# Edge layer of a four-layer graph network: the memset of an unused tile behind each of GpSimd's gathers is taken out

## The reference, cut to what matters

```python
h = maximum(layernorm(x), 0)
# _L2_gnn_ref(h, edge_index, edge_attr_64, W, b, gamma, beta):
msgs = concatenate([node_features[source], edge_features], axis=-1)   # 256 + 64 wide
msgs = silu(msgs @ W + b)
out = segment_sum(msgs, target, num_segments=n_nodes)
out = layernorm_0.001(out) * gamma + beta
x = x + out
```

## Time and profile before

| what | value |
|---|---|
| median of three runs | 7409.11 us |
| span of the profiled execution | 8931.6 us |
| span above the median | 1522.5 us |
| GpSimd busy | 5847.5 us, 65% of the span |
| TensorE matmuls busy | 5412.5 us, 61% |
| VectorE busy | 4963.7 us, 56% |
| ScalarE busy | 3871.5 us, 43% |
| granted TensorE clock, mean | 0.745 |
| DMA traffic | 894.72 MB, mean 100 GB/s |

### The profile page before, as it was taken

How to read it: one execution, slowest core, us unless ns; L and a number is a source line. 1 busy time by engine, 2 the same in 40 slices (tenths; PEclk the granted TensorE clock), 3 DMA queues, 4 the chain that set the end, 5 groups by cost and what they waited for, 6 DMA issues and landing times. The chain is left out here.

```text
span 8931.6 us, 130458 instructions
## 1 busy us (share of the span) xinstructions
PE 5412.5 (61%) x23088; PEld 4000.6 (45%) x23089; DVE 4963.7 (56%) x11653; ACT 3871.5 (43%) x9075; POOL 5847.5 (65%) x8186
## 2 busy tenths in 40 slices
PE   6442365666535656664676666658888754666665
PEld 5431244444424444443455555435555533444443
DVE  6444355555545555554677777744444445555556
ACT  2220255455424554552244444335555533454444
POOL 0555677777747777775467666657777765777774
PEclk9555677777767777776788988868888866777777
DMA  4112233333313333331466666423333323333332
GB/s 143 49 49 52 75 95 95 95 96 95 86 44 97 96 95 95 96 97 33 127 176 178 177 176 175 129 64 99 100 101 100 101 53 101 99 99 99 98 98 74
DMA packets 580940, 894.72 MB, mean 100 GB/s; under 512 B 307359, under 2 KB 357708, under 8 KB 580448
## 3 DMA queue, kind: packets, MB, share of 16 engines
q0 software_dynamic: 245984, 649.30, 26.7%
q1 hardware_dynamic: 334448, 218.84, 8.9%
q10 hardware_dynamic: 416, 25.60, 0.9%
HBM read 859.36 MB, written 59.47 MB: 103 GB/s over the span
## 5 line engine op out<-in xcount | busy, mean ns | idle before, releaser
L2002 POOL DMA_INDIRECT ad_ring<-tab_qv,ad_idx x808 | 770.7, 954 | 506.4 <-issue 217.6
L1515 POOL DMA_INDIRECT at_ring_0a<-tab_s,at_idx_0a x808 | 774.3, 958 | 430.9 <-PE at_po_0a L1680 219.2
L2396 POOL DMA_INDIRECT ae_ring<-tab_a,ae_idx x808 | 777.9, 963 | 423.0 <-PE ae_po L2553 233.7
L1515 POOL DMA_INDIRECT at_ring_0b<-tab_s,at_idx_0b x808 | 772.8, 956 | 426.7 <-PE at_po_0b L1680 213.2
L1515 POOL DMA_INDIRECT at_ring<-tab_s,at_idx x808 | 780.1, 965 | 377.6 <-PE at_po L1680 183.0
L1680 PE MATMUL at_po_0a<-at_rows_0a,at_hot_0a 128*128 128x264 f32 x1616 | 625.6, 560 | 520.8 <-ACT at_hr_0a L1780 199.8
L1680 PE MATMUL at_po_0b<-at_rows_0b,at_hot_0b 128*128 128x264 f32 x1616 | 624.3, 559 | 512.2 <-ACT at_hr_0b L1780 201.7
L1680 PE MATMUL at_po<-at_rows,at_hot 128*128 128x260 f32 x1616 | 614.5, 553 | 444.5 <-DVE acc L1566 179.0
L1680 PEld LDWEIGHTS at_po_0a<-at_rows_0a,at_hot_0a 128*128 128x128 f32 x1616 | 439.3, 282 | 670.8 <-DVE acc L1566 262.0
L1680 PEld LDWEIGHTS at_po_0b<-at_rows_0b,at_hot_0b 128*128 128x128 f32 x1616 | 438.5, 282 | 662.4 <-DVE acc L1566 264.4
L1680 PEld LDWEIGHTS at_po<-at_rows,at_hot 128*128 128x128 f32 x1616 | 435.9, 280 | 586.2 <-DVE acc L1566 225.4
(11 more groups left out here) (508 smaller groups left out, 14085.4 us busy)
## 6 DMA issues: line engine op xcount, KB each, us to landing
at_rr_0a<-relrow_d SPq DMA_DIRECT2D x102, 256.0 KB
at_rr_0b<-relrow_d SPq DMA_DIRECT2D x102, 256.0 KB
ad_rr<-relrow_d SPq DMA_DIRECT2D x102, 256.0 KB
at_rr<-relrow_s SPq DMA_DIRECT2D x102, 256.0 KB
ae_feat<-attr_pad SPq DMA_DIRECT2D x808, 32.0 KB
rnk_lrow<-lorow_f SPq DMA_DIRECT2D x98, 256.0 KB
attr_pad<-in_edge_attr_dram ACTq DMA_DIRECT2D x1, 25000.0 KB, 79.1
at_ring_0a<-tab_s,at_idx_0a POOLq DMA_INDIRECT x808
```

Source lines behind the costliest of these rows:

```text
L1515: eng.indirect_dma_start(out=ring[:, t.slot * STEP + u, :], out_offset=None, in_=table, in_offset=bass.IndirectOffsetOnAxis(ap=idx[:, t.sl ...
L2002: eng.indirect_dma_start(out=ring[:, t.slot * STEP + u, :], out_offset=None, in_=table, in_offset=bass.IndirectOffsetOnAxis(ap=idx[:, t.sl ...
L2396: eng.indirect_dma_start(out=ring[:, k, :], out_offset=None, in_=table, in_offset=bass.IndirectOffsetOnAxis(ap=idx[:, k:k + 1], axis=0))\
```

## The change

The tile `pause`, the semaphore `paused`, its wait and the 808 memsets are taken out. Nothing else is touched; gathers, their order and their other waits stay.

```diff
@@ aggregate_edges
-            pause = sb(f"ae_pause_{tag}", [P, STEP, P], F32, c)
@@
-            paused = ph.sem("ae_paused")
@@ @block.gpsimd
                     def gather(i, quads):
-                        eng.wait_ge(paused, i * STEP + STEP)
                         for q in range(quads):
                             eng.wait_ge(copied, i * (STEP // QUAD) + q + 1)
                             eng.wait_ge(summed, i * HALF + (q * 2 + 2))
@@
                                 eng.indirect_dma_start(out=ring[:, k, :], out_offset=None, in_=table,
                                                        in_offset=bass.IndirectOffsetOnAxis(ap=idx[:, k:k + 1], axis=0))\
                                     .then_inc(landed[k], 16)
-                                eng.memset(pause[:, k, :], 0.0).then_inc(paused, 1)
-
-                    eng.sem_inc(paused, STEP)
+
                     with eng.Fori(0, TURNS - 1) as i:
```

## The result

The changed kernel takes 7316.3 us (median of 4 runs, 7312.02 to 7316.78), the kernel before 7407.38 us beside it (7399.68 to 7412.71). The ratio is 0.9876, 95% interval 0.9863 to 0.9890: 91 us faster. I had forecast 7375 us, and 7335 us as the low end of the range.

What follows compares the result with a forecast made beforehand. GpSimd's gather cadence was held likelier than not to pace timed runs, though the profiled edge layer was bound by TensorE, VectorE and ScalarE. Half of 69 us, 34 us, off 7409 gave 7375 us; 8-in-10 range 7335 to 7445 us.

Steps and rivals of the forecast that it cites:

- the balance: Five edge passes: GpSimd's sequence without waits, 5767 us, nearly fills the estimated 5793 us, so GpSimd likely paces timed runs.
- "no change" rival: Edge layer: TensorE's loop paces timed runs too, GpSimd just waits 1.36 us a turn more; 7409 us, chance 0.27.
- The step: Edge layer, gather to gather on GpSimd: 1.345 to 1.26 us without the memset, 69 us over 808 gathers.
- The wait for `paused` "costs nothing": Edge layer, once a turn: it asks for memsets the same engine has done in order, so removing it gains nothing.
- Half of 69 us: Edge layer: gain between 0 and 69 us, the other engines' reserve unknown, so half was taken, 34 us.
- The 17.6 us that I had added up for TensorE: Edge layer: TensorE's four quads and sixteen transposes a turn at 2.4 GHz, without waits between engines.
- The low end: Whole kernel: 7335 us, the lower bound of the 8-in-10 range, just beyond the full gain.
- The clock rival: Seam of two edge-layer turns: longer quiet puts more of a turn at 1.2 GHz; 7435 us, slower, chance 0.23.
- a step of the clock, 56 us: Edge layer: denser TensorE raises its clock 0.81 to 0.87, 1.1 us a turn, 56 us; left out of the sum.
- Longer gathers: Edge layer: gathers without a memset between take 1.063 us, step 1.363 us, up to 7423 us; chance 0.05.
- What I said the profile would show: Edge layer: step 1.26, gap 0.30, gather 0.96 us; waits on sums about 300 us; layer within 10 us of before.
- Wrong in kind if the layer itself becomes shorter by more than 20 us: Edge layer in the profile: stated sign that the forecast is wrong in kind, a shortening of more than 20 us.

Runs made afterwards that it cites:

- second profile: The kernel before, profiled once more with no edit, after the 8931.6 us execution used for the prediction: 7396.4 us.
- all_out: Changed kernel with the memsets of the three attention passes, their tile, semaphore and waits taken out too: 7284.8 us, 0.9839.
- quad_wait: Kernel before with all memsets kept, but each quad waits for the memsets of a turn ago, not the last issued: 7361.3 us, 0.9943.
- seam_only: Changed kernel plus one memset a turn behind its last gather, and the wait for it at the next turn's start: 7341.9 us, 0.9923.
- Light_chain: Changed kernel with three of four "project" products of each edge-layer quad left out, all gathers kept: 7294.0 us, 0.9858.
- half_gathers: Changed kernel with every second gather of the edge layer left out, its rows staying zero: 7314.1 us, 0.9882.

## Why the prediction was wrong

*Who paces.* For the edge layer the balance was right. In the second profile the five passes take 5871 us from first to last gather, 104 us more than GpSimd's bare sequence of 5767 us, and in the edge layer 1126.5 us against 1087: the difference is the stall. But that GpSimd's sequence fills a pass doesn't say how near the next limit is: in the attention passes it filled them too, and the same edit bought next to nothing (all_out). The second profile has 1.5 us of waits for the sums where the first had 233.7. The "no change" rival, which rested on those waits, fell with them.

*The step.* 1.345 to 1.26 us, 69 us, was the forecast; 1.346 to 1.263 and 67 us is what came. Its parts (gap 0.16 to 0.17 behind a memset, 0.30 behind a gather) hold.

*The wait for `paused` "costs nothing".* This step failed. It costs 0.79 us a turn, 39.5 us: quad_wait took it away alone (39.7 us), and seam_only put it back. I argued that the engine had done those memsets in order. In the first profile the gather at the turn's start waited for TensorE, and that longer wait covered this one. I should have worked the turn's start out once more for a run in which TensorE's wait is gone. The code shows the case: with the 16 that are added ahead of the loop, the wait for (i + 1) x 16 asks for the very last memset issued, with nothing between.

*Half of 69 us.* This failed too; half was a guess between two ends, worked out from no row. The other engines gave way almost to the end. GpSimd's sequence became 67 + 39.5 = 106 us shorter; 15 us were given back, since turns take 20.50 us in the mean where GpSimd would take 20.21 (0.29 x 50 = 15). 106 - 15 = 91 us is the gain in the runs, and 92 that of the layer. Light_chain, where that limit is gone, gets those 15 us: 105.9 us against the runs of before beside it, where the changed kernel has 91.1, and 16 us by the layer. Of the 57 us between the 34 forecast and the 91 measured, some 39.5 are the stall and 18 the half. The 17.6 us that I had added up for TensorE at full clock are not what a turn can do: at the clock granted, with the waits between engines, it is 20.3 (half_gathers).

*The low end.* 7335 us was the full step and a few us more. A range built from the step alone could not hold 7316.

*The clock rival* is wrong: in the layer it went from 0.88 to 0.90, and the layer became shorter. TensorE's wait for VectorE ahead of a product, about once a turn, did not grow: 1.84 us in the mean before (54 times), 1.85 after (51 times). Nor did a step of the clock, 56 us, come on top: the layer's clock rose by 0.02, and before the change the turn was GpSimd's whatever the clock. *Longer gathers*: 0.963 to 0.958 us, wrong in sign.

*What I said the profile would show*: gap, step and gather came as said. The waits on the sums (about 300 us forecast, 28.3 measured) and the layer (within 10 us; it fell by 92 from the second profile) did not, as both leaned on the first profile. "Wrong in kind if the layer itself becomes shorter by more than 20 us" is what happened.

## What to carry to other kernels

Set the profiled execution beside the timed runs first. If it is a fifth longer, as here, don't take its waits for those of the timed runs; GpSimd's durations could still be used, and its sequence added up without waits named the right limit of the edge layer. A wait for the memset just issued on the same engine was a stall here, although the order of the instructions made it true, and a longer wait at the same place hid it: work out what such a wait costs with the longer one gone. Before the pacing engine's work is cut, look how far the next limit is: here 91 of 106 us came out in one layer, and 5 or 4 us of some 150 in each of two attention passes.

## What the hardware showed that I had not expected

Gathers that GpSimd issued one behind the other were 1.25 to 1.26 us apart from start to start, in every pass that has no memsets. A memset of 0.117 us between two of them adds nothing, since the gap behind it and the gap of the bare pair make up the same 0.30 us (0.117 + 0.19); one of 0.220 us adds 0.083, one of 0.33 us another 0.107.

A wait for GpSimd's own memset just issued left the engine idle for 0.95 us instead of 0.17, and as long when the memset was 0.33 us (45.5 us in 48 waits in both kernels). For the memset that lies twelve before the last one it was the plain 0.16, and a bare increment in the memset's place added nothing. What the engine does in the 0.95 us no run here shows.

One profiled execution took 8931.6 us and the next of the same kernel 7396.4 us, with GpSimd's instructions as long in both and the layer's clock at 0.81 and 0.88. The clock alone doesn't account for it: the other engines' loop took 20.3 us at 0.90 (after), and if all of it went with the clock it would be 22.6 us at 0.81, an estimate; the first profile has 26.3 a turn. What the rest is was not found.
